# Experts' weights in quarters, waits for the experts' stores moved to the gathers, last turn and last residual in halves

## The reference, cut to what matters

```python
xn = layernorm(x)
x = x + attention(xn) * silu(down(silu(gate(xn)) * up(xn)))
xn = layernorm(x)
# s: project to v and x2; 3-tap filter on v; FFT over the sequence, times the
#    spectrum of an implicit filter (an MLP of the position), back; times x2; project
s = hyena(xn)
# y: probs = softmax(gelu(xn @ wg1) @ wg2); top 2 of 20; y += p_e * (xn @ We[e] + be[e])
g = silu(mixture(xn))
x = x + s * g
```

## Time and profile before

| | us |
|---|---|
| median of 3 runs | 1047.89 |
| lowest and highest | 1044.74 and 1056.45 |
| the profiled execution, in all | 1041.73 |
| its span, first to last instruction | 1040.0 |
| mean granted TensorE clock in the span | 0.981 |

### The profile page before, as it was taken

How to read it: one execution, slowest core, us unless ns; L and a number is a source line. 1 busy time by engine, 2 the same in 40 slices (tenths; PEclk the granted TensorE clock), 3 DMA queues, 4 the chain that set the end, 5 groups by cost and what they waited for, 6 DMA issues and landing times. The chain is left out here.

```text
span 1040.0 us, 19172 instructions
## 1 busy us (share of the span) xinstructions
PE 935.8 (90%) x5936; PEld 713.9 (69%) x5936; DVE 715.2 (69%) x1459; ACT 483.4 (46%) x888; POOL 341.6 (33%) x610
## 2 busy tenths in 40 slices
PE   1889999999999999999999989863999899999995
PEld 1666876776775775775776765653666688888884
DVE  8566477677677677677677467370575359999997
ACT  1445555555555555545545546541223244444441
POOL 7213412713713613613613524522000073333310
PEclk9999999999999999999999999986999999999998
DMA  5875935535634634634544620477667554343321
GB/s 182 155 167 88 185 145 83 126 142 77 129 142 71 135 142 64 139 145 63 111 154 63 138 79 3 173 237 246 208 204 223 166 171 131 123 123 122 123 61 41
DMA packets 88172, 137.23 MB, mean 132 GB/s; under 512 B 9971, under 2 KB 63411, under 8 KB 86068
## 3 DMA queue, kind: packets, MB, share of 16 engines
q1 hardware_dynamic: 69620, 101.27, 40.1%
q0 software_dynamic: 6144, 16.79, 5.3%
q10 hardware_dynamic: 12352, 18.48, 5.1%
HBM read 79.88 MB, written 55.57 MB: 130 GB/s over the span
## 5 line engine op out<-in xcount | busy, mean ns | idle before, releaser
L1501 DVE TENSOR_REDUCE Mneg<-PS 128x2 f32<-128x1024 f32 (+2 forms) x192 | 194.7, 1042 | 59.8 <-PE PS L997 58.6
L1259 ACT ACTIVATE PT<-PS 128x512 f32<-128x512 f32 (+1 forms) x384 | 172.6, 529 | 114.0 <-PE PS L1021 112.2
L1757 POOL TENSOR_TENSOR idle_p<-neghalf 128x1 f32<-128x1 f32 x128 | 25.1, 196 | 297.0 <-ACT PT L1259 297.0
L993 PE MATMUL PS<-ks,qs 96*128 96x256 f32 (+3 forms) x512 | 117.5, 338 | 3.2 <-issue 2.1
L1021 PE MATMUL PS<-qs,ks 96*128 96x512 f32 (+3 forms) x512 | 117.7, 348 | 2.2 <-ACT PT L1259 1.2
L1021 PEld LDWEIGHTS PS<-qs,ks 96*128 96x128 f32 x512 | 85.4, 188 | 35.5 <-ACT PT L1259 17.7
L816 PE MATMUL PS<-xnT,Wgu 128*128 128x512 f32 x384 | 103.1, 410 | 3.0 <-ACT V L1204 2.4
L1934 PE MATMUL PS<-Wes,xbT 128*128 x336 | 97.0, 398 | 2.8 <-issue 1.6
L1763 POOL TENSOR_SCALAR_AFFINE_SELECT PT<-PT 128x256 f32<-128x256 f32 x256 | 98.7, 409 | 0.0
L1035 PE MATMUL PS<-PT,V 128*32 128x512 f32 (+3 forms) x1024 | 85.5, 440 | 3.9 <-POOL PT L1763 3.1
L816 PEld LDWEIGHTS PS<-xnT,Wgu 128*128 128x128 f32 x384 | 70.0, 191 | 25.9 <-issue 7.1
(11 more groups left out here) (229 smaller groups left out, 1662.5 us busy)
## 6 DMA issues: line engine op xcount, KB each, us to landing
qs<-qk_parts SPq DMA_DIRECT2D x96, 128.0 KB
ks<-qk_parts SPq DMA_DIRECT2D x96, 128.0 KB
slots_out<-yb ACTq DMA_DIRECT2D x28, 384.0 KB, 3.2
xb<-slots_in SPq DMA_DIRECT2D x83, 128.0 KB, 2.4
qk_parts<-qhl SPq DMA_DIRECT2D x16, 512.0 KB, 2.7
qk_parts<-khl SPq DMA_DIRECT2D x16, 512.0 KB, 3.1
xn2T_parts<-xn2T SPq DMA_DIRECT2D x8, 1024.0 KB, 4.9
xT<-xn2T_parts ACTq DMA_DIRECT2D x7, 1024.0 KB, 4.8
```

The costliest lines, as they stand in the source:

```text
L993: pe.matmul(out, qs[:, hd, P * qt:P * qt + P], ks[:, hd, 0:keys], start=n % a_bank == 0, stop=False, skip_group_check=True)
L1259: act.activation(PT[:, g % 2, j, 512 * n:512 * n + width], PS[:, 4 + n, 0:width], ACT.Exp, scale=SCALE).then_inc(S["exped"], 1)
L1501: dve.tensor_reduce(out=Mneg[:, 0, qt, heads[0]:heads[-1] + 1], in_=all_of, op=ALU.max, axis=AX.X, negate=True).then_inc(S["maxed"], 1)
```

## The change

1. `EACH` quarter of the experts (there are five, of four experts) gets a semaphore of its own, `e_in[quarter]`, which counts its two pieces of weights and its piece of biases. TensorE and VectorE wait for quarter q before block 4q.
2. SP loads eight pieces of weights and two of biases in the first program, and the other two and three in the second, behind blocks 2 to 9. Each expert gets at least one block (`ALU.max` with P), so that block n is of an expert up to n.
3. In the last batch only one part of the spectrum is made within the attention. Part (0,1) comes behind the transposes of the heads, (1,0) and (1,1) behind the output projection. The copies are shared between ScalarE and VectorE, and the repair of the first row is at the end of VectorE's list.
4. The residual of the last batch runs by halves, with the statistics behind each half.
5. `next_rows_T` for batch 1 moves from the first program to turn 4 of the second.
6. SP no longer waits for the stores of the experts' results; ScalarE and GpSimd wait for them at the start of the third program.
7. In the last turn of the convolution Z's mixed half is split by halves, `back_mixed` runs by halves, and so do the output's bias, the result's rows and their store.

```diff
-        w_e = sem("w_e"); b_in = sem("b_in")
+        EACH = 4
+        e_in = [sem(f"e_in{n}") for n in range(NE // EACH)]
+        E_IN = 16 * (CC + 1)
...
+        SPECTRUM_BANK = {(0, 0): 0, (0, 1): 4, (1, 0): 6, (1, 1): 7}
...
+        def back_mixed_halves(pe, b):
+            for half in range(2):
+                pe.wait_ge(U["z_lo"], 2 * b + 2 + half)
+                for m in range(CC):
+                    for c in (2 * half, 2 * half + 1):
...
+        def split_z_high_half(act, b, half):
+            act.wait_ge(U["dstep"], ND * b + ND - 1 + half)
...
-                for n in range(4):
-                    load_experts(sp, n, 1)
-                sp.wait_ge(S["ont"], B)
-                load_biases(sp, 0, 3)
-                load_experts(sp, 4, 1)
-                load_biases(sp, 1, 4)
+                load_experts(sp, 0)
+                sp.wait_ge(e_in[0], 16)
+                load_experts(sp, 1)
+                sp.wait_ge(e_in[0], 32)
                 store(B - 1)
-                load_experts(sp, 5, 1)
-                load_experts(sp, 6, 1)
+                load_experts(sp, 2)
+                sp.wait_ge(e_in[1], 16)
+                load_experts(sp, 3)
+                store_T(B - 1)
                 sp.wait_ge(S["x1_out"], 16 * B)
                 sp.wait_ge(S["ln2_done"], NT * B)
-                load_biases(sp, 2, 0)
-                load_experts(sp, 7, 1)
-                store_T(B - 1)
-                load_biases(sp, 3, 1)
-                load_experts(sp, 8, 1)
-                load_biases(sp, 4, 2)
-                load_experts(sp, 9, 1)
+                load_biases(sp, 0)
+                for n in range(4, EARLY_PIECES):
+                    sp.wait_ge(e_in[(n - 1) // CC], 16 * ((n - 1) % CC + 1))
+                    load_experts(sp, n)
+                load_biases(sp, 1)
...
-                SPECTRUM = {(NG, 1): (0, 0), (NG, 2): (0, 1), (NG, 4): (1, 0), (NG + 1, 0): (1, 1)}
+                SPECTRUM = {(NG, 1): (0, 0)}
...
                     heads_as_rows(b, last)
                     if not last:
                         project_v(b + 1, (2, 3))
+                    else:
+                        filter_spectrum(0, 1)
                     output_transposes(b)
...
                     project_out(b)
+                    if last:
+                        filter_spectrum(1, 0)
+                        filter_spectrum(1, 1)
...
                         act.activation(Win[:, HI, :, :], st_win[:, :, :], ACT.Copy).then_inc(t_hi, 1)
+                        spectrum_imaginary(0)
                     split_output(b)
...
                 act.activation(Inv[:, HI, :, :], st_i[:, :, :], ACT.Copy).then_inc(t_hi, 1)
+                spectrum_real(1)
+                spectrum_imaginary(1)
                 projected(act, 0, (0, 1))
...
-                next_rows_T(act, 1)
...
+                def residual_halves(b):
+                    dve.wait_ge(S["xres_in"], 16 * (b + 1))
+                    for n in range(2):
...
+                        dve.tensor_tensor(flat, PS[:, 2 + n, :], flat, ALU.mult).then_inc(S["y_sb"], 1)
+                        dve.wait_ge(S["y_sb"], 2 * b + n + 1)
+                        add = dve.tensor_tensor(xres[:, part, :], xres[:, part, :], G[:, part, :], ALU.add)
...
+                        for t in (2 * n, 2 * n + 1):
+                            last = dve.bn_stats(st[:, t, :], xres[:, t, :])
...
                     if last:
-                        dve.wait_ge(h_sb, 6)
-                        dve.tensor_copy(HN[0:1, :, 0, :], HB[0:1, :, 0, :]).then_inc(h_fix, 1)
-                        dve.wait_ge(h_fix, 1)
-                        dve.memset(HB[0:1, :, 0, :], 0.0)
+                        spectrum_first()
...
                 block_tables()
+                spectrum_ends()
...
                     load_block(sp, n, row, after=n - AHEAD + 1)
+                    if n == 2:
+                        load_biases(sp, 2)
+                    if n == 4:
+                        load_experts(sp, 8)
+                    if n == 5:
+                        load_experts(sp, 9)
+                    if n == 7:
+                        load_biases(sp, 3)
+                    if n == 9:
+                        load_biases(sp, 4)
                     if n == AHEAD:
                         sp.dma_start(bo2b[:, :], bo2.partition_broadcast(P)).then_inc(U["wo_in"], 16)
                 sp.wait_ge(U["wo_in"], 32)
-                for h_ in range(2):
-                    sp.wait_ge(yb_out[h_], 16 * NI)
...
+                        if RING * i + u < NE and (RING * i + u) % EACH == 0:
+                            pe.wait_ge(e_in[(RING * i + u) // EACH], E_IN)
...
+                def rows_in_turn(i, last=False):
+                    turn(i, last)
+                    if i == 4:
+                        next_rows_T(act, 1)
...
             @block.scalar
             def _(act):
+                for h_ in range(2):
+                    act.wait_ge(yb_out[h_], 16 * NI)
...
                     else:
-                        split_z_low(dve, b, 1)
+                        split_z_low_half(dve, b, 0)
+                        split_z_low_half(dve, b, 1)
+                        second_choice(dve, b)
+                        branch_out(dve, b - 1, (1,))
+                        gated(dve, b)
                         result_rows(dve, b - 1)
...
+                        for half in range(2):
+                            branch_out(dve, b, (half,))
+                            result_half(dve, b, half)
...
                 pool.memset(vt[:, :, T + 1:T + 2], 0.0).then_inc(U["edges"], 1)
+                for h_ in range(2):
+                    pool.wait_ge(yb_out[h_], 16 * NI)
```

More of the change, by code:

```diff
@@ L313, in transform_part @@
                     for i, j in PAIRS:
-                        last = pe.matmul(PS[:, bank + 2 * half + part, C * (q_ % 2):C * (q_ % 2) + C],
+                        last = pe.matmul(PS[:, bank, C * (q_ % 2):C * (q_ % 2) + C],
                                          Fwd[:, i, kc, P * q_:P * q_ + P], src[:, j, 2 * half + kc, :],
@@ L324, in transform @@
                 for part in range(2):
-                    transform_part(pe, src, bank, half, part, done)
+                    transform_part(pe, src, bank + 2 * half + part, half, part, done)
         ND = 20
@@ L373, in back_whole @@
                          lambda j, c: Inv[:, j, c, :], NQ, stop=False)
+        def back_mixed_halves(pe, b):
[3 more added lines that the diff above has]
+                    for c in (2 * half, 2 * half + 1):
+                        for n, (i, j) in enumerate(PAIRS):
+                            last = pe.matmul(PS[:, 6 + m, T // 2:T], Zs[:, i, 1, c, P * m:P * m + P],
+                                             Inv[:, j, c, 0:T // 2], start=False, stop=half == 1 and c == 3 and n == 2,
+                                             skip_group_check=True)
+                    if half == 1:
+                        last.then_inc(U["y_ps"], 1)
         def back_mixed(pe, b):
@@ L526, in program @@
         FILTER_PARTS = 7
+        EARLY_PIECES = 8
         def filtered(dve, b):
@@ L540, in gated, with branch_out @@
                 dve.tensor_tensor(o32[:, m, :], PS[:, 6 + m, :], x2_of(b, m), ALU.mult).then_inc(U["o_sb"], 1)
-        def branch_out(dve, b):
-            for n in range(2):
+        def branch_out(dve, b, halves=range(2)):
+            for n in halves:
                 dve.wait_ge(U["s_ps"], 2 * b + n + 1)
@@ L562, in pe_turn @@
                 transposes(pe, b + 1)
-            back_mixed(pe, b)
-            if not last:
+            if last:
+                back_mixed_halves(pe, b)
+            else:
+                back_mixed(pe, b)
                 forward(pe, b + 1)
@@ L964, in filter_spectrum @@
                         pe.wait_ge(t_lo, 1)
-                    transform_part(pe, v2, 0, half, part, f_ps)
+                    transform_part(pe, v2, SPECTRUM_BANK[half, part], half, part, f_ps)
                 def unit(b, g, u):
@@ L1278, in attention @@
                             silu_of_gate(b + 1, 1)
-                        if s == NG + 1 and last:
-                            filter_spectrum()
                         if s <= NG:
@@ L1970, in before @@
                     load_block(act, 1, row)
-                in_turns(act, before, turn)
+                in_turns(act, before, rows_in_turn)
                 store(NBLK - 1)
@@ L1993, in turn @@
                             pos_in_blocks(dve, i - 2)
-                def before():
-                    dve.wait_ge(b_in, 16 * NE // EACH)
-                in_turns(dve, before, turn)
+                in_turns(dve, lambda: None, turn)
         cursor[0] = wes_at
@@ L2059, in _ @@
                         load_x1(sp, n + 2)
-                for e in range(2):
-                    sp.wait_ge(X["stored"][e], 16 * B // 2)
+                for half in range(2):
+                    part = slice(2 * half, 2 * half + 2)
```

(12 more changed lines are left out.)

102 lines of the change are left out of this document (71 added, 31 removed).

## The result

The changed kernel runs in 1044.47 us in the median of 20 runs (1041.18 to 1050.14), the kernel before beside it in 1049.51 us (20 runs): a ratio of 0.9959, 95% interval 0.9941 to 0.9978. Two later measurements gave 0.9939 (0.9910 to 0.9968) and 0.9944 (0.9918 to 0.9970). So the change saves 4 to 6 us, 0.5%, where 13.4 were forecast. It is well under the 1% that a measurement was said to tell, and the time lies above the range of 1028 to 1043. Ratios are of fast runs alone, medians of all runs of a kernel.

A forecast was written before the change was run, and what follows sets the result against it. TensorE, 90% busy, idles at the three programs' ends and waits for SP's loads early in the second. -8.8+2.3-2.2-2.1-2.2-0.4 = -13.4 gives 1028.3 us against the profiled execution, 1034.5 for the median; range 1028 to 1043.

The forecast's parts named there:

- First program, -8.8: First program's end: it ends with VectorE at 706.1, first block load at 708.2 instead of 717.03, 8.8 us saved.
- Rival C: SP's queue or the last scatter's landing still ends the first program, about 710; total -9.4, 1038.5 us; chance 0.17.
- SP being done before VectorE: First program's end: at 5 us per late piece, SP issues its last near 702, ahead of VectorE's 706.1.
- (a): Last attention step, first program: spectrum pieces moved out bring the output projection 1.2 us sooner.
- The residual by halves: First program, last batch: 1.3 us less, 0.4 lost to queueing; normalised rows ready 2.1 us sooner with (a).
- (c): First program: two spectrum pieces ahead of the input projection start it 1.4 us later; routing, scatters and tables shift +0.6.
- Second program, +2.3: Second program's start: five late issues ahead of block 10 cost 2.1 us, slower block landings 0.2.
- the rows: nothing: Second program, turn 4: ScalarE issuing the next batch's rows costs nothing, as it waits for TensorE in most turns.
- rival D: Second program starved by late pieces: block loads report behind five transfers, 20 us instead of 2.3; 1052.2 us; chance 0.04.
- Second barrier, -2.2 and -2.1: Between second and third programs: barrier opens 2.2 us sooner without SP's wait; TensorE keeping 2.4 GHz saves 2.1.
- Rival B: TensorE's clock falls at the second barrier all the same; total -11.3, 1036.6 us; chance 0.2.
- End, -2.2 and -0.4: Third program's end: splitting into halves ends the chain at 1034.4 instead of 1036.60, -2.2; smaller last store, -0.4.

The follow-up runs named there:

- Experiment 1: Changed kernel plus two more 128 KB scatters, read by nobody, behind GpSimd's last eight in the first program; 1076.59 us in a single run, slower chip.
- experiment 7: Changed kernel with GpSimd's low part of the in-projection weights held until the residual's first half is added; 1044.08 us, ratio 0.9951 to the kernel before.
- experiment 9: Changed kernel with SyncE again waiting for the result stores at the second program's end, on a quicker chip; 1045.34 us, ratio 0.9978 to the kernel before.
- number 8: Changed kernel with the third program's end whole again (one split, residual and store per batch); 1046.83 us, ratio 0.9966 to the kernel before.
- numbers 1 to 3: Changed kernel, slower chip, in turn: two extra scatters, 1076.59 us; batch 1's rows loaded in the first program, 1075.37; all weights and biases loaded there, 1077.41.
- number 4: Changed kernel with SP again waiting for the result stores at the second program's end, on the slower chip; 1068.96 us, ratio 0.9992 to the kernel before.

## Why the prediction was wrong, and where it was right

**First program, -8.8: the end was mis-sized.** The prediction let it end with VectorE at 706.1, which is 54.2 us after L314, plus the barrier. It ends 58.0 to 58.9 us after L314 in the five undisturbed profiles of changed kernels, 4.5 to 5.4 us less than in the profile predicted from, where 8.8 less were forecast. The sentence that failed is "The last scatter must have landed too; I estimate 707.5 for that": a landing like that of a block load, 2.1 to 2.8 us, was no measure of it, and even this 707.5 is later than the 706.1 that went into the sum. GpSimd's drain ends 5.3 to 6.7 us after the last scatter's issue in all profiles but the first of before (8.7, at 713.1). Rival C, which was given 0.17, named it as a cause and had its size as well: 710 is 58.1 us after L314, and its 4.8 us for the first program are what was measured. Experiment 1 shows that this end follows the scatters. The shortfall is one against the profile predicted from. Against the second profile of the kernel before, in which SP ended the program 6.7 us after the drain, the gain is 7.4 to 8.3 us: how much SP's wait was worth differs from one execution to the next, and two profiles don't tell its mean. SP being done before VectorE was right (707.50; the four pieces behind store_T were issued 4.8 us apart, 5 forecast), and so was (a): the output transposes and the projection came 1.4 us earlier against L314 (1.2 forecast). The residual by halves gave 0.7 instead of 2.1 with (a), since one addition met GpSimd's operation (experiment 7). In (c) the projection started 0.6 us later against L314 (1.4 forecast, though 676.1 against 674.78 is 1.3), the split of xn2T came 0.1 us earlier instead of 0.9 later, and the last scatter 0.4 earlier instead of 0.6 later. Neither matters to the end beside the drain.

**Second program, +2.3: the first half of it held, "the rows: nothing" failed.** Up to block 16 the shift against the two profiles of before (30.0 and 29.6) is 1.6 to 2.6 us, at 31.6 to 32.2. So the five issues cost about what they were put at, and rival D, with 20 us, is out. The last sentence of that part, that ScalarE waits for TensorE in most turns and so the rows of batch 1 cost nothing, looked at who issues and not at what the megabyte stands ahead of: VectorE's buffers of results come free only when the stores behind it have landed, and the store at 765.61 took 7.5 us for that instead of the median 3.2. This step cost 3.0 us on average (119.8 over the six profiles with the rows in turn 4, 116.8 over the two with SyncE). About 1 us of the +3.2 that remain without the rows (116.8 against 113.6, the mean of before's two) I haven't explained.

**Second barrier, -2.2 and -2.1: right on the quicker chips.** 0.99 instead of 3.21 us from the last store's issue, and the clock kept; experiment 9 puts them at 2.25 and 1.7 to 2.7. Rival B is out there.

**End, -2.2 and -0.4: right.** Counted from the restart, the last addition ends 2.2 us sooner in the kernel after than in number 8 (200.3 and 202.5), and from there to the end of the span it takes 2.7 instead of 3.4 us; together 2.2 to 3.2 over the profiles, 2.6 forecast.

The sum in the forecast's own terms, from mean lengths of the undisturbed profiles against the first profile of before: 58.5-63.4 = -4.9; 119.8-113.0 = +6.8; -2.2; 203.5-208.6 = -5.1; in all -5.4. (The mean lengths are those of the table, without the profiles of kernels that undo the stretch in question.) The three ratios give -4.3, -6.4 and -5.9. Against the second profile of before the same sum is -8.7, so the agreement with the ratios is in part luck of the profile chosen, and it leaves out the profiles marked with a star. The two failed steps, 3.9 and 4.5 us, less 0.4 more than forecast in the third program, are the shortfall of 8.0.

Two things stay open. The clock fell at 664 us, behind the first edit that acts, in three of the eight profiles of changed kernels on the quicker chips and in neither of the two of before, and cost 4.7 us ahead of the last scatters each time. Whether the change makes this fall more frequent, and so eats part of the gain, no run tells. And on the slower chip the third program took 221 to 222 us in numbers 1 to 3 and 213.4 in number 4, with TensorE idle behind "issue" for 1 to 2 us at a time near 870 us and its clock at 0.50 afterwards. No profile of the kernel before was taken there, so I can't say whether the change provokes this; the ratios of numbers 2 and 4 (1.0037 and 0.9992) would fit.

## What to carry to other kernels

Before crediting the removal of the engine that ends a program last, list the drains of all engines on the program's closing line: they show who is second and by how much, and a scatter issued by GpSimd keeps its drain open well past its issue (5.3 to 8.7 us here) although every engine looks idle. A transfer moved into a "waiting" engine's queue must be priced by what is queued behind it: its landing delays the stores that free buffers. And a single profile is one draw of the clock; compare lengths from the last untouched point, not times from the start.

## What the runs showed of the hardware that I had not expected

- GpSimd's drain at the end of the first program lasts until 5.3 to 6.7 us (once 8.7) after the issue of its last 128 KB scatter, while the drains of the other engines take 0.01 to 2.3 us on the quicker chips. It ends 3.0 to 4.4 us after the scatters' last packet. At the end of the second program, where its last scatter lies far back, it adds nothing: TensorE restarts 0.99 us after the last store's issue.
- VectorE's addition of two SBUF tiles (0.69 us alone) ended 0.57 us after GpSimd's running tensor operation of 2.4 us, both times they met.
- With no edit near it, TensorE's granted clock fell at 614 to 624 us in nine of ten profiles on the quicker chips and in some of them again at 628 or 653. L314 came 3.5 to 8.8 us later for it than in the first profile of before, the tenth.
